# Narrow attention: the second iteration's query gets its own place and is made directly behind the first's

## The reference, cut to what matters

```python
x = x + L1_xattn(_layernorm(x), ctx, ctx, w_proj, b_proj)            # q, k, v unprojected
x = x + L1_ffn(_layernorm(x), ...)
x = x + L2_xattn(_layernorm(x), ctx, ctx, mask, wq, wk, wv, wo, bo)  # with a mask over keys
x = x + L2_ffn(_layernorm(x), ...)
x = x + L3_xattn(_layernorm(x), ctx, ctx, Wq, bq, Wk, bk, Wv, bv, Wo, bo)
x = x + L3_ffn(_layernorm(x), ...)
# a narrow attention:
qh, kh, vh = proj(q), proj(k), proj(v)          # 16 heads of 8
scores = einsum(qh, kh)                          # per head 256 x 64
out = einsum(softmax(scores / sqrt(8)), vh) @ Wo + bo
```

## Time and profile before

| | before |
|---|---|
| median of three runs | 1924.78 us |
| profiled execution, its own time | 1917.87 us |
| its span | 1916.1 us |
| TensorE busy in it (PE) | 1569.3 us |
| VectorE, ScalarE, GpSimd busy | 1270.2, 898.6, 203.6 us |
| granted TensorE clock, mean of the span | 0.90 of 2.4 GHz |
| narrow attention, first stage | from 322.85 |
| second, third stage | from 791.98, 1521.52 |

### The profile page before, as it was taken

The page is one execution under the profiler, slowest core; times in us unless marked ns, Lnnn a source line. Parts: engine busy times, 40 slices in busy tenths (PEclk is TensorE's granted clock), DMA queues, the critical chain, the costliest instruction groups (busy, mean ns, idle before and its releaser), DMA issues. The chain is left out here.

```text
span 1916.1 us, 26161 instructions
## 1 busy us (share of the span) xinstructions
PE 1569.3 (82%) x8251; PEld 1048.2 (55%) x8251; DVE 1270.2 (66%) x2824; ACT 898.6 (47%) x1679; POOL 203.6 (11%) x184
## 2 busy tenths in 40 slices
PE   6999979788799999788948999999999879857005
PEld 5777755555466666455636666566666445523004
DVE  4777774586576676567656665666665558677985
ACT  3655642576455555456623222232222167627752
POOL 2100010112000000111410000000000111010410
PEclk9999985699799999899979999999999969958557
DMA  4000000321000000142100000000000022100001
GB/s 157 1 1 0 0 1 3 121 51 34 1 1 1 0 0 1 37 159 58 42 1 0 1 1 1 1 0 0 1 1 0 3 63 51 34 1 0 0 0 44
DMA packets 23374, 41.71 MB, mean 22 GB/s; under 512 B 7709, under 2 KB 11165, under 8 KB 22238
## 3 DMA queue, kind: packets, MB, share of 16 engines
q1 hardware_dynamic: 23262, 40.32, 7.1%
HBM read 19.32 MB, written 2.10 MB: 11 GB/s over the span
## 5 line engine op out<-in xcount | busy, mean ns | idle before, releaser
L973 DVE TENSOR_REDUCE mP_a<-psY_a 128x8 f32<-128x512 f32 x192 | 128.0, 687 | 106.6 <-PE psY_a L811 106.3
L731 ACT ACTIVATE probs_a<-psX_a 128x512 f32<-128x512 f32 x192 | 108.9, 595 | 134.1 <-PE psX_a L838 133.5
L1726 ACT ACTIVATE xsh_f<-xs_f 128x512 fp32r<-128x512 f32 x120 | 75.8, 632 | 197.8 <-DVE xs_f L1979 197.7
L1979 DVE TENSOR_TENSOR xs_f<-xT_f,psR_f 128x512 f32<-128x512 f32 x128 | 86.9, 686 | 78.4 <-PE psR_f L1798 74.4
L1842 PE MATMUL psX_f<-xs_f,wo_f2w 128*128 128x512 f32 x256 | 128.6, 594 | 0.0
L2374 PE MATMUL ps_f<-wT_f,xq_f 128*128 128x128 f32 x192 | 24.3, 290 | 125.5 <-DVE xq_f L2395 125.5
L1979 DVE TENSOR_TENSOR xs_f<-aoT_f,psR_f 128x512 f32<-128x512 f32 x128 | 85.8, 685 | 61.7 <-PE psR_f L1798 61.4
L1506 DVE SCALAR_TENSOR_TENSOR g_f<-psU_f,cols_f1w,t_f 128x512 f32<-128x512 f32 (+1 forms) x104 | 77.9, 749 | 72.8 <-ACT t_f L1319 71.1
L811 PE MATMUL psY_a<-ks_a,xs_a 96*128 96x256 f32 x384 | 99.3, 362 | 18.6 <-DMA xs_a<-ql_a 17.3
L1401 PE MATMUL psO_f<-h_f,w_f1w 128*128 128x512 f32 (+1 forms) x208 | 107.6, 599 | 0.0
L1319 ACT ACTIVATE t_f<-psU_f,cols_f1w 128x512 f32<-128x512 f32 (+1 forms) x104 | 71.2, 684 | 76.4 <-PE psU_f L1385 76.4
(11 more groups left out here) (435 smaller groups left out, 4161.5 us busy)
## 6 DMA issues: line engine op xcount, KB each, us to landing
xs_a<-qh_a SPq DMA_DIRECT2D x192, 64.0 KB, 2.0
xs_a<-ql_a SPq DMA_DIRECT2D x96, 64.0 KB, 2.0
x_sb<-in_x SPq DMA_DIRECT2D x1, 2048.0 KB, 8.6
out<-x_sb SPq DMA_DIRECT2D x1, 2048.0 KB, 6.3
w_f1w<-in_F_w SPq DMA_DIRECT2D x2, 792.0 KB
ctxT<-in_ctxT SPq DMA_DIRECT2D x1, 1024.0 KB, 12.6
maskf_a<-in_mask SPq DMA_DIRECT2D x8, 128.0 KB, 2.2
maskf_a<-in_maskT SPq DMA_DIRECT2D x8, 128.0 KB, 2.6
```

Source lines behind the costliest of these rows:

```text
L731: nc.scalar.activation(probs[:, b % 2, g, :, :], psX[g % 2][:].rearrange("p (e t) -> p e t", e=2), ACT.Exp, scale=float(dv) ** -0.5).then_ ...
L973: nc.vector.tensor_reduce(mP[:, b % 2, h // 2, col:col + 8], psY[h % 2][:].rearrange("p (h k) -> p h k", h=8), axis=AX.X, op=ALU.max).then ...
L1726: nc.scalar.activation(xsh[:, e % RING, :], xs[:, e % RING, :], ACT.Copy).then_inc(s("x_high").sem, 1)
L1979: nc.vector.tensor_tensor(xs[:, e % RING, :], src, psR[e % 2][:], ALU.mult).then_inc(s("scaled").sem, 1)
```

## The change

- Query 1 is written to its own place, the groups 2 and 3 of `probs[:, 1]` (`q_parts`); batch 1's exponentials for these groups wait until its transfers have landed. All other queries use `qh` and `ql` as before.
- Iterations of even and odd number count their transfers on semaphores of their own (`stacked0` to `stacked3`).
- SP issues `ahead.start` behind stack(1) instead of behind stack(0); in the second stage the mask load of iteration 1 comes between stack(0) and stack(1).
- TensorE's start becomes x(0), q(0), k(0), x(1), q(1), k(1), scores(0,0), v(0), scores(0,1), scores(0,2), scores(0,3), max_T(0).
- ScalarE's start becomes xT(0), qh(0), the four key rows, xT(1), one of the copies of `kmax`, qh(1), the values, the other three copies, max_rows(0).
- VectorE's start becomes ln(0), keys_low(0), xn(0), keys_low(1), ln(1), ql(0), xn(1), mask, ql(1), then the maxima as before with ln(2) between them, and xn(2).

```diff
+        def q_parts(j):
+            if j == 1:
+                return tuple(probs[:, 1, g, :, :].rearrange("p e t -> p (e t)").bitcast(F32R) for g in (2, 3))
+            return qh[:], ql[:]
+        def stacked(j, half):
+            return s(f"stacked{half + 2 * (j % 2)}")
+        def wait_stacked(eng, j, half):
+            eng.wait_ge(stacked(j, half).sem, stacked(j, half).at(96 * (j // 2 + 1)))
...
                 stack(j)
-                if not j:
+                if j == 1:
                     ahead.start(pr, sp)
...
             def front_q(j):
                 act.wait_ge(s("q_proj").sem, s("q_proj").at(j + 1))
-                if j:
+                if j >= 2:
                     for half in range(2):
-                        act.wait_ge(s(f"stacked{half}").sem, s(f"stacked{half}").at(96 * j))
-                nc.scalar.activation(qh[:], psF[:], ACT.Identity, bias=cols[:, 0:1]).then_inc(s("q_ready").sem, 1)
+                        wait_stacked(act, j - 1 if j > 2 else 0, half)
+                nc.scalar.activation(q_parts(j)[0], psF[:], ACT.Identity, bias=cols[:, 0:1]).then_inc(s("q_ready").sem, 1)
...
+                if b == 1 and g >= 2:
+                    for half in range(2):
+                        wait_stacked(act, 1, half)
...
             front_x(0)
             front_q(0)
+            front_k(0, range(4))
+            front_x(1)
+            act.wait_ge(s("kmax").sem, s("kmax").at(16))
+            maxima_off(0, 0)
+            front_q(1)
             act.wait_ge(s("v_zeroed").sem, s("v_zeroed").at(1))
-            front_k(0, range(4))
             front_v(0)
-            act.wait_ge(s("kmax").sem, s("kmax").at(16))
-            for q in range(2):
-                for b in range(BPI):
-                    nc.scalar.activation(ks[MAXROW:P, q, b, :, :], probs[MAXROW:P, 0, :, 0, :], ACT.Copy)\
-                        .then_inc(s("kmax_ready").sem, 1)
-            front_x(1)
+            for n in range(1, 4):
+                maxima_off(n // 2, n % 2)
             max_rows(0)
-            front_q(1)
...
             front_k(0)
             pe.wait_ge(s("q_split").sem, s("q_split").at(1))
-            front_v(0)
+            front_x(1)
+            front_q(1)
+            pe.wait_ge(s("k_ready").sem, s("k_ready").at(4))
+            front_k(1)
             stacks(0, 0)
             scores(0, 0)
+            pe.wait_ge(s("q_split").sem, s("q_split").at(2))
+            front_v(0)
             stacks(0, 1)
             scores(0, 1)
-            pe.wait_ge(s("k_ready").sem, s("k_ready").at(4))
-            front_k(1)
-            pe.wait_ge(s("v_ready").sem, s("v_ready").at(1))
-            front_x(1)
             scores(0, 2)
             scores(0, 3)
             max_T(0)
-            front_q(1)
...
             front_ln(0)
-            for k in range(2):
-                keys_low(k)
+            keys_low(0)
             front_xn(0)
+            keys_low(1)
...
+            front_ln(1)
             front_q(0)
-            front_ln(1)
+            front_xn(1)
             if masked:
                 front_mask(0)
-            front_xn(1)
             dve.wait_ge(s("mP_zeroed").sem, s("mP_zeroed").at(1))
+            front_q(1)
             for h in range(2):
                 largest(0, h)
             front_ln(2)
             for h in range(2, 4):
                 largest(0, h)
-            front_q(1)
             front_xn(2)
```

More of the change, by code:

```diff
@@ L95 @@
     "front_out", "front_ready", "stats_ready", "probs_T", "normed", "summed",
-    "k_proj", "k_high", "kmax", "kmax_ready", "stacked0", "stacked1", "mP_zeroed", "v_zeroed", "v_proj", "k_spread", "k_ready", "max_T", "max_ready",
+    "k_proj", "k_high", "kmax", "kmax_ready", "stacked0", "stacked1", "stacked2", "stacked3", "mP_zeroed", "v_zeroed", "v_proj", "k_spread", "k_ready", "max_T", "max_ready",
     "ones_row", "scores_T", "bv_ready", "bv_proj",
@@ L648, in stack @@
                 sp.wait_ge(s("q_split").sem, s("q_split").at(j + 1))
+                high, low = q_parts(j)
                 for g in range(GROUPS):
-                    for r, part in enumerate((qh, qh, ql)):
+                    for r, part in enumerate((high, high, low)):
                         sp.dma_start(xs[GF * r:GF * r + GF, j % 2, g, :].bitcast(F32), part[GF * g:GF * g + GF, :].bitcast(F32))\
-                            .then_inc(s(f"stacked{g // 2}").sem, 16)
+                            .then_inc(stacked(j, g // 2).sem, 16)
             if masked:
@@ L737, in _, with maxima_off @@
                 act.wait_ge(s("bv_proj").sem, s("bv_proj").at(1))
+            def maxima_off(q, b):
+                nc.scalar.activation(ks[MAXROW:P, q, b, :, :], probs[MAXROW:P, 0, :, 0, :], ACT.Copy)\
+                    .then_inc(s("kmax_ready").sem, 1)
             front_x(0)
             front_q(0)
+            front_k(0, range(4))
[3 more added lines that the diff above has]
+            front_q(1)
             act.wait_ge(s("v_zeroed").sem, s("v_zeroed").at(1))
-            front_k(0, range(4))
             front_v(0)
-            act.wait_ge(s("kmax").sem, s("kmax").at(16))
-            for q in range(2):
-                for b in range(BPI):
-                    nc.scalar.activation(ks[MAXROW:P, q, b, :, :], probs[MAXROW:P, 0, :, 0, :], ACT.Copy)\
-                        .then_inc(s("kmax_ready").sem, 1)
-            front_x(1)
+            for n in range(1, 4):
+                maxima_off(n // 2, n % 2)
             max_rows(0)
-            front_q(1)
             for b in range(B):
@@ L815, in stacks @@
             def stacks(j, half):
-                pe.wait_ge(s(f"stacked{half}").sem, s(f"stacked{half}").at(96 * (j + 1)))
+                wait_stacked(pe, j, half)
                 pe.wait_ge(s("k_ready").sem, s("k_ready").at(4 * j + 4))
@@ L900, in _ @@
                 if not p and j + 2 < ITERS:
[L901 to L904, removed]
+                    pe.wait_ge(s("v_ready").sem, s("v_ready").at(j + 1))
                     front_x(j + 2)
@@ L961, in front_q @@
                 dve.wait_ge(s("q_ready").sem, s("q_ready").at(j + 1))
-                if j:
+                if j >= 2:
                     for half in range(2):
-                        dve.wait_ge(s(f"stacked{half}").sem, s(f"stacked{half}").at(96 * j))
-                nc.vector.scalar_tensor_tensor(ql[:], psF[:], cols[:, 0:1], qh[:], ALU.add, ALU.subtract)\
+                        wait_stacked(dve, j - 1 if j > 2 else 0, half)
+                high, low = q_parts(j)
+                nc.vector.scalar_tensor_tensor(low, psF[:], cols[:, 0:1], high, ALU.add, ALU.subtract)\
                     .then_inc(s("q_split").sem, 1)
@@ L1031, in narrow_attention @@
     n1 = ITERS
-    counts = dict(**ahead.counts, k_proj=2, k_high=2, k_split=2, kmax=16, kmax_ready=4, stacked0=96 * n1, stacked1=96 * n1, mP_zeroed=1, v_zeroed=1, ln_var=n1, ln_rstd=n1, ln_out=n1,
+    counts = dict(**ahead.counts, k_proj=2, k_high=2, k_split=2, kmax=16, kmax_ready=4, stacked0=48 * n1, stacked1=48 * n1, stacked2=48 * n1, stacked3=48 * n1, mP_zeroed=1, v_zeroed=1, ln_var=n1, ln_rstd=n1, ln_out=n1,
                   bias_added=n1, ln_T=n1, xT_ready=n1, q_proj=n1, q_ready=n1, q_split=n1, v_proj=n1, v_ready=n1, k_spread=n1,
```

## The result

The change makes the kernel faster: median 1895.78 us (1889.91 to 1898.50, 4 runs) against 1922.67 (1917.61 to 1929.26, 4 runs) for before, ratio 0.986 with a 95% interval of 0.9827 to 0.9894. That is 26.9 us, some 20 to 33. I had forecast 14.7; the rival "the clock rises early" said 24.2. The profiled execution took 1895.58 (before: 1917.87), 22.3 less. Of these, 25.1 come from the three narrow attention stages, measured from the issue of `kmax` to the start of the last addition to `x`. The part ahead of the first stage took 1.8 longer, the feed-forward parts 0.3 and the tail 0.8, with no change in them.

A forecast was written before the change was run, and what follows sets the result against it. It took the three attention stages' starts to be bound by DMA waits, queue order and TensorE's low clock. Stage gains 4.55, 4.15 and 4.2 plus clock 1.0 and 0.8 made 14.7: 1924.78 to 1910.1 us, range 1900 to 1921.

The forecast's parts named there:

- the clock rises early: Rival: all three narrow attention stages reach 2.4 GHz by batch 1, gaining 24.2 us, to 1900.6; chance 0.17.
- The "1.45" of batch 1: First stage, batch 1: scores(2,1) follows scores(2,0) by 0.6 us instead of 2.04, without the DMA wait, gaining 1.45.
- "2.15", 1.1 and 1.5: Forecast gains in us at max_T(0), the first batch's transpose of maxima, in the first, second and third stages.
- not earlier: First stage: scores(0,0) start at 339.4 us against 339.42 before, since q(1) and k(1) now stand ahead of them.
- I take about a fifth of each, 1.0 and 0.8: Extra us in the first and third stages from an earlier clock rise, out of possible 3.7 plus 1.9, and 3.4.
- nearer the low one: Second stage: gain taken as 4.2 us, between 3.0 with the low clock throughout and 6.5 with the high one.
- 5.55, 4.2 and 4.95: Forecast gains in us of the first, second and third stages, clock terms of 1.0 and 0.8 included in first and third.
- the 5.4 of my high bound: Second stage with the high clock: the batch-1 step of 15.1 us shrinks by 5.4, for a gain of 6.5.
- The row of 310 to 315 us: Profile row before the change: TensorE busy 5.00 of 5.00 us, clock at 0.50; cited against filled waits raising the clock.
- what the start gains is kept to the end of the stage: Steady loop: same instructions as before, so the start's gain in a stage, 4.55 us in the first, is not lost.
- Only the stalls go: Rival: VectorE's late ln(2) and ScalarE's queue eat the start, max_T(0) no earlier; gain 7 us, to 1917.7; chance 0.22.
- The clock stays low: Rival: early batches never lift the clock, costing 1.9 us a batch; four more in each stage make 1936; chance 0.06.

The follow-up runs named there:

- experiment 10: Kernel after the change, with VectorE's mask conversion for the next iteration moved ahead of ln and xn (second stage only): 1887.37 us, ratio 0.9821 to before.
- Experiments 1 and 2: First: experiment 1. Second: that kernel with idle matmuls filling TensorE's wait ahead of scores(2,0) in the first and second stages: 1903.03 us, ratio 0.99 to before.
- experiment 1: Kernel after the change, with the weight loads again behind stack(0), ahead of stack(1): 1906.13 us, ratio 0.9914 to before.
- experiment 5: Kernel before the change, with three idle matmuls in TensorE's waits, two ahead of scores(0,0) and one ahead of scores(0,1): 1918.75 us, ratio 0.9984 to before.
- experiment 3: Kernel before the change, with only the weight loads moved behind stack(1): 1919.06 us (1895.70 to 1936.70), ratio 0.995 to before.
- experiments 10 to 12: Three runs: experiment 10; it plus the idle matmuls of experiment 6, 1886.12 us; that plus ln(2) early and a filler behind q(2), 1884.59 us.
- experiment 7: Kernel after the change, with ln(2) on VectorE moved behind only the first of the maxima: 1899.20 us, ratio 0.989 to before.
- experiment 6: Kernel after the change, with two idle matmuls on TensorE, one behind v(0) and one before max_T(0): 1896.99 us, ratio 0.9877 to before.

## Why the prediction was right and wrong

**The bound and the waits: right.** The DMA waits at scores(2,0), scores(2,1) and the mask are gone, stack(1) goes directly behind stack(0), xn(0) is 1.7 us sooner (1.6 forecast), and the steady steps of the first and third stage are unchanged. The "1.45" of batch 1 was the right stall.

**max_T(0): right, with the clock's phase on top.** "2.15", 1.1 and 1.5 were 3.37, 1.86 and 3.93. I had every operation at the low clock from the first projection on, and scores(0,0) therefore "not earlier". They came 2 us earlier, since the clock fell at T 10.8 instead of 7.5. That is not the edit's doing alone: experiment 10 has the same first stage, there it fell at 7.0, and max_T(0) stood at 23.68, close to the 23.3 of the forecast. So some 1.6 of the 3.37 are luck of this execution.

**The clock: the step that failed.** It is "I take about a fifth of each, 1.0 and 0.8" and, in the second stage, "nearer the low one". The rival's condition (2.4 GHz by batch 1) came true in all three stages. By max_T(2) or (3) the forecast had 5.55, 4.2 and 4.95; measured were 11.15, 7.2 and 9.8 (by the stages' ends 14.4, 2.5 and 8.3). The largest part is step 1 to 2 in the first and third stage, 4.46 and 4.43 us. Of that I had put 1.45 and 1.7 to the stall, and of what the low clock costs I took a fifth. Experiments 1 and 2 show why they hang together: the low clock behind the stall came with the wait, and went when the wait was filled. I had taken them as two terms, the second at a discount, where taking away the wait takes away both. In the second stage this step shrank by 6.1, past the 5.4 of my high bound.

The row of 310 to 315 us had made me doubt that a busy TensorE would rise at all. It shows a stretch that stayed low and no more: the kernel before had 2.4 GHz from T 34.9 to 38.3, and lost it at the wait that the change removes. That "the other two stages stayed at 1.2 GHz at this point", and that the first stage's batch 1 was "dense and slow", had overlooked these 3.4 us. Why TensorE stays low in such a stretch is not explained by any run. It is longer than the row: from 290 to 320 us of before it is busy all the time.

```profile
290.00:320.00 30.00, 30.00 (x84) 16.74 (x83) 10.86 (x39) 6.83 (x15) 0.00 (x0) 0.50 0.00 1
```

**What was given back.** The second stage lost 4.7 us to three clock falls in its loop; I had said that "what the start gains is kept to the end of the stage". And of the first stage's 14.4 us, 3.2 arose at its very end, where no work differs: before, the products of the last heads ran at the low clock. The two windows of before show the clock falling at each of them; those at the same place after do not:

```profile
474.00:477.00 3.00, 3.00 (x27) 1.41 (x30) 0.42 (x1) 0.60 (x1) 0.00 (x0) 0.50 0.00 0
...
480.00:483.00 3.00, 2.95 (x28) 1.64 (x32) 0.42 (x1) 0.66 (x1) 0.00 (x0) 0.60 0.02 5
```

```profile
464.00:467.00 3.00, 3.00 (x40) 1.94 (x41) 0.61 (x2) 1.19 (x2) 0.00 (x0) 1.00 0.01 3
...
470.00:473.00 3.00, 1.65 (x32) 0.74 (x24) 1.53 (x2) 0.00 (x0) 0.00 (x0) 1.00 0.02 5
```

In the third stage the same place cost 1.5 the other way.

**The rivals.** "Only the stalls go" is out by max_T(0). "The clock stays low" is out for the start. As a mechanism it was half right, in another place: the second stage's loop. Its price of 1.9 us a batch is not that of a step at 1.2 GHz: the clock was low for only 5.9 of the 10.19 us of the step it was read from.

**The parts.** Taken out one by one, late weights are worth about 10 us, the early query 14, the place of its own 6 to 10, the keys' order 4. These are differences of medians and of ratios, each uncertain by some 9 by the intervals, so the last two are not told apart from nothing by the totals. They add up to more than 27, since taking out either of the first two brings the stall, and the clock's fall with it, back.

**Open.** The loop of the second stage falls into its rhythm in some kernels and not in others, with the same instructions and the same waits for the mask. Order alone does not decide it: before and experiment 1 stay clear of it, experiment 5, with the order of before, does not. What decides it was not settled. A good part of a total's spread goes with the clock: in experiment 3 the shortest execution, 1895.70 us, had a mean granted clock of 0.911, the longest, 1936.70, one of 0.888. Where in the program these falls were can't be told, since only one execution of each kernel has a trace.

## What to carry to other kernels

A wait of TensorE in the middle of a dense loop can cost its own length and then the low clock behind it, so price a stall as both: here 2.9 and 2.5 us. When a start-up is shortened, look whether the loop behind it has a wait that the clock can fall at, and take that away as well (the mask conversion here, 9.4 us of a stage for two moved lines). Small transfers that a near step needs are to be issued ahead of bulk loads on the same queue; then look at the next ones, since the stall may only have moved on (experiment 3). When two kernels have equal totals, compare their stages: experiment 5 gained 8.8 us in two of them and lost 12.5 in the third.

## What the runs showed that I had not expected

- With a wait of 1.30 us for the mask in each second step, the clock can fall again and again, 20.5 us apart, 1.56 us a time, or not at all. Without the wait there was no fall in the loop (experiments 10 to 12).
- Time gained ahead of a dense stretch can be worth nothing: the 1.2 us of experiment 7, and those of step 0 to 1 in experiment 6, were lost again to falls of the clock.
- The clock's phase, with the same instructions, is worth 3.2 us at one stage's end and 1.6 at a stage's start.
